# Two products with half as many stationary columns, an unrolled loop and a fifth mask on GpSimd in a four-layer graph kernel

## What is computed

```python
# layer 2, per head
logits = q @ k.T / sqrt(32) + log(clip(adj, 1e-8, None))
attn   = softmax(logits);  out = attn @ v
# layer 3, per head
logits  = q @ k.T / sqrt(32) + (2 * adj - 1)
weights = softmax(logits) * (0.25 + 0.75 * adj)
weights = weights / sum(weights);  attended = weights @ v
```

## Time and profile before

| | |
|---|---|
| median of three runs | 4772.2 us (4770.67 to 4772.46) |
| profiled execution, its own time | 4770.8 us |
| its span, first to last instruction | 4769.0 us |
| TensorE busy | 4307.2 us, 90% |
| VectorE busy | 3509.2 us, 74% |
| ScalarE busy | 2024.3 us, 42% |
| GpSimd busy | 1895.1 us, 40% |
| L618, 4096 records | 1132.9 us busy |
| L597 and L584, 2048 each | 659.2 and 657.1 us busy |
| L1324 on GpSimd, 512 | 1303.5 us busy, 2547 ns each |
| L1055 on VectorE, 512 | 767.3 us busy, 1501 ns each |

### The profile page before, as it was taken

How to read it: one execution, slowest core, us unless ns; L and a number is a source line. 1 busy time by engine, 2 the same in 40 slices (tenths; PEclk the granted TensorE clock), 3 DMA queues, 4 the chain that set the end, 5 groups by cost and what they waited for, 6 DMA issues and landing times.

```text
span 4769.0 us, 60615 instructions
## 1 busy us (share of the span) xinstructions
PE 4307.2 (90%) x16432; PEld 2005.4 (42%) x16432; DVE 3509.2 (74%) x4722; ACT 2024.3 (42%) x3638; POOL 1895.1 (40%) x1064
## 2 busy tenths in 40 slices
PE   7998899988999889998899898998989989899898
PEld 5523264232743337432374323743237332463324
DVE  3798748987489864898648986488855888558893
ACT  3264432544335443354423644235442354424543
POOL 1164602646026450264502645036440365404553
PEclk9998999989999899998999999999999999999999
DMA  3201102011020110201101011110111101111010
GB/s 104 67 18 32 49 23 59 18 32 49 25 59 16 34 47 28 56 16 34 47 32 53 15 34 47 33 53 14 36 47 34 49 14 36 49 36 47 14 35 16
DMA packets 109021, 179.63 MB, mean 38 GB/s; under 512 B 28256, under 2 KB 51040, under 8 KB 108704
## 3 DMA queue, kind: packets, MB, share of 16 engines
q1 hardware_dynamic: 108704, 175.89, 12.8%
HBM read 83.12 MB, written 8.39 MB: 19 GB/s over the span
## 4 chain that ended last, share of the span: by engine, by line
PE 59%; issue 17%; POOL 14%; DVE 7%; ACT 2%; POOLq 0%; DMA 0%; SPq 0%; DVEq 0%; ACTq 0%
PE ps L618 11%; PE ps L514 11%; POOL region_p L1324 9%; PE ps L560 9%; PE ps L506 8%; PE ps L597 6%; PE ps L584 6%; PE ps L707 5%; PE ps L550 2%; DVE row_max L1063 2%; POOL rstd L1336 1%; POOL v_head L1318 1%; DVE region_p L1055 1%; DVE sums_t L1034 1%; POOL y_t L1389 1%
## 5 line engine op out<-in xcount | busy, mean ns | idle before, releaser
L1324 POOL TENSOR_TENSOR region_p<-region_p,mask 128x1024 f32<-128x1024 f32 x512 | 1303.5, 2547 | 733.8 <-ACT region_p L827 733.6
L827 ACT ACTIVATE region_p<-ps 128x512 f32<-128x512 f32 x2048 | 1111.3, 595 | 907.8 <-PE ps L584 905.5
L1063 DVE TENSOR_REDUCE row_max<-ps 128x1 f32<-128x1024 f32 x1024 | 1213.5, 1214 | 42.7 <-PE ps L597 41.6
L618 PE MATMUL ps<-region_p,v_head 128*64 128x512 f32 x4096 | 1132.9, 634 | 74.4 <-POOL region_p L1324 30.2
L1055 DVE TENSOR_TENSOR region_p<-region_p,mask 128x1024 f32<-128x1024 f32 x512 | 767.3, 1501 | 67.3 <-ACT region_p L827 66.3
L597 PE MATMUL ps<-region_k,region_q 96*128 (+1 forms) x2048 | 659.2, 411 | 57.8 <-DVE row_max L1063 53.1
L584 PE MATMUL ps<-region_q,region_k 97*128 (+1 forms) x2048 | 657.1, 401 | 3.7 <-ACT region_p L827 1.1
L560 PE MATMUL ps<-values,region_k 128*128 128x256 f32 x2048 | 475.7, 387 | 0.0
L1336 POOL TENSOR_TENSOR rstd<-var_eps,minus_half 128x2 f32<-128x2 f32 (+1 forms) x160 | 119.5, 747 | 880.1 <-DVE var_eps L1015 880.1
L597 PEld LDWEIGHTS ps<-region_k,region_q 96*128 (+1 forms) x2048 | 130.1, 100 | 723.4 <-issue 459.6
L618 PEld LDWEIGHTS ps<-region_p,v_head 128*64 128x64 f32 x4096 | 208.9, 138 | 520.2 <-issue 393.4
(11 more groups left out here) (148 smaller groups left out, 4493.6 us busy)
## 6 DMA issues: line engine op xcount, KB each, us to landing
mask<-in_adj SPq DMA_DIRECT2D x64, 512.0 KB, 7.8
mask<-in_adj_t SPq DMA_DIRECT2D x64, 512.0 KB, 3.2
y_t<-o_raw SPq DMA_DIRECT2D x256, 64.0 KB, 2.0
sums_t<-o_raw SPq DMA_DIRECT2D x256, 64.0 KB, 2.0
region_q<-region_p SPq DMA_DIRECT2D x192, 64.0 KB, 2.0
region_k<-region_p SPq DMA_DIRECT2D x192, 64.0 KB, 2.0
region_q<-sums_t SPq DMA_DIRECT2D x192, 64.0 KB, 2.0
region_k<-sums_t SPq DMA_DIRECT2D x192, 64.0 KB, 2.0
```

The source lines that it names most:

```text
L618: last = nc.tensor.matmul(ps[64 * c:64 * c + 64, 6 + i, :], v_head[i][:, t, :], probs[:, t % RING, c * HALF:(c + 1) * HALF], start=(t == 0 ...
L827: nc.scalar.activation(probs[:, t % RING, c * HALF:(c + 1) * HALF], ps[:, 4 + c, :], ACT.Exp, scale=DK ** -0.5).then_inc(exp_done, 1)
L1063: nc.vector.tensor_reduce(row_max[i][:, t:t + 1], flat[:, (t % 2) * N:(t % 2 + 1) * N], AX.X, ALU.max)\
L1324: nc.gpsimd.tensor_tensor(p, p, mask[:, t, :], ALU.mult).then_inc(masked_pool, 1)
```

## The change

Both kinds of score product are split into two of 64 stationary columns, one for PSUM partitions 0 to 63 and one for 64 to 127, with the same moving operand. TensorE's loop over pairs of heads becomes unrolled code; the loops of the other engines stay. GpSimd masks tiles 0, 2, 3, 5 and 7 and VectorE tiles 1, 4 and 6; the copy of the next head's values so comes after tile 2. Which mask `with_values` and `make_mask3` wait for follows from the two tuples.

```diff
-POOL_TILES = (1, 3, 5, 7)
+POOL_TILES = (0, 2, 3, 5, 7)
...
                         pe.wait_ge(exp_done, att(b, layer, h, 2 * T, 2 * t + c - 1))
-                        nc.tensor.matmul(ps[:, 4 + c, :], k_aug[0:AUG, number(h), t * P:(t + 1) * P],
-                                         q_aug[0:AUG, number(h), c * HALF:(c + 1) * HALF],
-                                         start=True, stop=True).then_inc(st_done, 1)
+                        for m in range(2):
+                            last = nc.tensor.matmul(ps[64 * m:64 * m + 64, 4 + c, :],
+                                                    k_aug[0:AUG, number(h), t * P + 64 * m:t * P + 64 * m + 64],
+                                                    q_aug[0:AUG, number(h), c * HALF:(c + 1) * HALF],
+                                                    start=True, stop=True)
+                        last.then_inc(st_done, 1)
...
                 for c in range(2):
-                    last = nc.tensor.matmul(ps[:, 2 * (t % 2) + c, :], q_aug[0:AUG - 1, number(h), t * P:(t + 1) * P],
-                                            k_aug[0:AUG - 1, number(h), c * HALF:(c + 1) * HALF],
-                                            start=True, stop=True)
+                    for m in range(2):
+                        last = nc.tensor.matmul(ps[64 * m:64 * m + 64, 2 * (t % 2) + c, :],
+                                                q_aug[0:AUG - 1, number(h), t * P + 64 * m:t * P + 64 * m + 64],
+                                                k_aug[0:AUG - 1, number(h), c * HALF:(c + 1) * HALF],
+                                                start=True, stop=True)
                 last.then_inc(nat_done, 1)
...
-                with pe.Fori(1, H // 2 - 1) as pair:
+                for pair in range(1, H // 2 - 1):
                     for i in range(2):
                         head(b, layer, (pair, i), i, True)
```

## The result

The changed kernel takes 4710.9 us, median of four runs (4708.0 to 4715.6), against 4772.3 before (4770.7 to 4773.1). The ratio is 0.9874, 95% interval 0.9861 to 0.9887. The forecast was 4710 us. The profiled execution took 4708.0, its span is 4706.2, 62.8 less than before.

What follows compares the result with a forecast made beforehand. TensorE was taken to bound six of eight heads, VectorE and GpSimd the last two. 5.1 + 0.5 - 0.7 - 1.05 gave 3.9 us a layer, x 16 = 62 off 4772.2: 4710 us, range 4670 to 4750.

Steps and rivals of the forecast that it cites:

- five heads: Steady heads of an eight-head layer: each goes from 16.23 to 15.20 us, stall of 0.62 included; 5.1 a layer won.
- head 0: A layer's first head: three steps lack value products, five save 0.235 each, less a stall of 0.62; 0.5 us won.
- start of a layer: 64-column score products alternating with 128-column L506: 4 x 0.235 more, some 0.2 hidden by a VectorE wait; +0.7 us.
- last two heads: End of a layer, bounded by VectorE and GpSimd: +2.1 us in the first layer, 0 in the second.
- The step: TensorE's work per 128-row tile: 1.98 to 1.745 us, the 0.235 where 128 and 64 columns meet gone.
- The loads: Stationary loads of the split products, doubled in number: exposure taken as nothing, bounds nothing and 0.06 us a pair.
- (c): Doubled loads in front of split products make a pair 0.276 and the step 1.98 again: 4799 us; chance 0.11.
- (d): Gap around L618 comes from something else of fp32 on 64 columns and stays: about 4790 to 4800 us; chance 0.05.
- (e): Split bf16 score halves run one after the other, 2.59 us a step: about 5250 us; chance 0.03.
- (b): GpSimd's copy takes 0.9 us, two maxima are late, a head comes to 15.75: 4756 us; chance 0.08.
- (a): TensorE sets the pace throughout, no maximum is late, a head takes 14.57 us: 4647 us; chance 0.12.
- Cost of unrolling: zero: TensorE's unrolled loop over pairs of heads: no cost, bounds 0 and 1.0 us a layer, 16 in all.

Runs made afterwards that it cites:

- experiment 2: Kernel before the change with GpSimd masking tiles 0, 2, 3, 5, 7, nothing else: 4801.4 us, ratio 1.0051.
- experiment 4: Changed kernel with GpSimd masking tiles 1, 3, 5, 7 and the scores for the maximum whole again, only transposed scores split: 4758.1 us, ratio 0.9969.
- experiment 9: Changed kernel with GpSimd masking tiles 1, 3, 5, 7 and both halves for the maximum written to PSUM partitions 0 to 63: 4929.6 us, one run.
- experiment 1: Kernel before the change with TensorE's loop over pairs of heads unrolled, nothing else: 4749.9 us, ratio 0.9956.
- experiment 5: Changed kernel with ScalarE's fourth preparation of a next mask placed after tile 7 of the eighth head, not tile 6: 4694.9 us, ratio 0.9837.
- experiment 6: Changed kernel with GpSimd masking tiles 1, 3, 5, 7 and the split products for the maximum ordered m outside, c inside: 4647.7 us, ratio 0.9736.

## Why the prediction was right, and where it was not

**The sum.** Per layer, by the table of stretches:

| term | forecast | measured (first, second layer) |
|---|---|---|
| five heads | -5.15 | -5.02, -5.06 |
| head 0 | -0.5 | -0.76, -1.55 |
| start of a layer | +0.7 | +1.05, +1.10 |
| last two heads | +2.1, 0 | +3.06, +0.21 |
| net, mean of both | -3.9 | -3.49 |

Over the 16 layers that is -80.6 for -82 in the five heads, -18.5 for -8 in head 0, +17.2 for +11 at the start and +26.2 for +17 in the last two heads: -56 for -62, and 7 us from stretches that the sum didn't touch. Every term has the sign that was forecast, and the errors of the smaller ones cancel in part. That the total meets 4710 within 1 us is luck.

In medians, unrolling alone is -23.6, the splits on top of it -97.7 and the fifth mask on top of both +58.8 (-62.5; the change itself is -61.4). These parts hold for this order only. The 20 us that unrolling wins in the tails are there with four masks and not with five: with five masks the tails are 35.9 and 30.9 in the loop (experiment 2) and 36.3 and 31.1 unrolled (the changed kernel).

**The step** was forecast at 1.745 and is 1.73. The gap went where the forecast had it: 0.43 into the value product instead of 0.52, 0.86 out of it instead of 1.01, and experiment 4 shows nearly all of it (0.22) as soon as one kind of product has 128 columns again. That both kinds had to be split together was right. The loads of the stationary operand show what happens at the change of columns (before, then after):

```profile
477.01 0.20 PEld L618 LDWEIGHTS ps<-region_p,v_head 128*64 128x64 f32 x4 [0.42 <-issue]
```

```profile
465.53 0.36 PEld L623 LDWEIGHTS ps<-region_p,v_head 128*64 128x64 f32 x4
```

Before, the load for L618 starts together with its product (477.01), 0.31 after the last L584 has started. After, it starts 0.21 ahead of its product (465.74), while the product in front still runs. Out of the value product it is the same: the load and the product of L597 start together before (476.04 and 476.05), and the load of L601 runs 0.42 ahead after (466.18 and 466.60). In experiment 4 the load that isn't taken ahead is that of L585 (470.12, with its product), and L621's is again 0.21 ahead. At the border to L506 the load is 0.21 ahead before (404.61 for 404.82) and starts with its product after (403.89 for 403.90). At each of these changes of columns the load isn't taken ahead.

**Side by side** was taken from the fp32 value product alone; experiment 9 shows it for bf16. **The loads** cost nothing, as taken. The page's groups:

```profile
L601 PEld LDWEIGHTS ps<-region_k,region_q 96*64 96x64 bf16 x4096 | 204.8, 114 | 660.8 <-DVE row_max L1068 409.2 <-issue 211.2 <-DMA region_k<-region_p 14.3
L585 PEld LDWEIGHTS ps<-region_q,region_k 97*64 97x64 bf16 x4096 | 238.0, 113 | 383.5 <-ACT region_p L832 160.4
```

A half load takes 113 to 114 ns, the whole one took 102. Two of them one after the other, 0.23 a pair, would be more than the 0.216 of the products. They aren't taken one after the other: 4096 loads of 114 ns would be 467 us, and L601's are busy for 204.8, so the two halves' loads run at once. The Trainium skill (TensorEngine Tiling (Array Packing), Restrictions and Gotchas) has it that column tiling turns off fast weight load. The trace agrees in sign only: the load is 11 ns longer for half of the columns, but not the 138 of the fp32 one, and no run shows a cost of it. Rivals (c), (d) and (e) fell with the step; (b) had two late maxima a head, and there is one; (a) had none behind VectorE's stretched mask, and even with four masks the head stops at 14.97, not 14.57, since VectorE's queue is full.

**The head** came out at 15.18 for 15.20, with the one stall of 0.58 for 0.62 behind VectorE's mask of tile 4, as laid out. The rules read from the earlier trace rows (a VectorE mask and a GpSimd mask exclude each other, reductions from PSUM and GpSimd masks don't) carried it. No run tests them other than through such durations.

**Unrolling** is a term that failed, by a small amount. "Cost of unrolling: zero" had a bound for a loss and none for a gain. The some 0.21 between L605 and L597, which the forecast took as the transpose's own time, held 0.06 to 0.07 of the loop. That is 5 us, and the changed kernel has them. The 20 us of the tails in experiment 1 go with the granted clock, and the changed kernel doesn't have them. Whether the split products could have stayed in the loop wasn't tried.

**The last two heads of the first layer** were mis-sized twice. The earlier trace rows is from graph 0, and there the tail is 31.77; in six of eight graphs it is 33.7, because ScalarE's wait of experiment 5 is in them already. These are the graphs in which the clock is full in the middle of the tail; graphs 0 and 7 have neither the full clock nor the wait. The trace of before has it in a later graph (the columns are those of the timeline):

```profile
2115.62 1.15 ACT L815 ACTIVATE mask_exp<-mask,minus_ones 128x1024 f32<-128x1024 f32 x1 [2.31 <-DVE mask L1045]
```

"All eight look alike" was an assumption. In experiment 1 the wait is in no graph (31.8 in six of eight), but unrolled code doesn't remove it by itself: experiment 4 is unrolled and has it in seven of eight graphs, at 1.9 to 2.1 us, with a mean clock of 0.86 in the same stretch and the half clock a little later in it. With the fifth mask it is in all eight and longer, 4.47 for 2.31, and the forecast's working had only VectorE's and GpSimd's queues in it, not ScalarE's. From step 0 of the seventh head the forecast had 34.96 to 37.1; it was 36.9 to 39.4 in the typical graph, so the difference of 2.1 was near 2.5 with both ends wrong. **The second layer** was 34.2 in the forecast and is 34.14 (516.38 to 550.52), GpSimd's masks without a gap:

```profile
525.03 24.43 POOL L1329 TENSOR_TENSOR region_p<-region_p,mask 128x1024 f32<-128x1024 f32 x8
```

Eight masks at 3.05 each: one alone takes 2.36, so each spends some 0.7 behind VectorE's. That this tail costs nothing is in part the clock again: in the stretch from 14 to 26 us after the last transpose it is 0.72 in seven of eight graphs before and 1.00 in all after. With four masks and a full clock there is one graph, in experiment 4, and its tail is 28.7, not 31. How the zero divides between the mask and the clock isn't shown.

**The start** cost 1.1 instead of 0.7. The rows that answer to the earlier trace rows:

```profile
402.91 1.05 PE L601 MATMUL ps<-region_k,region_q 96*64 96x512 bf16 x8 [0.20 <-DMA region_k<-region_p]
403.90 2.00 PE L506 MATMUL ps<-w_v,y_t 128*128 128x256 f32 x8
405.82 0.62 PE L601 MATMUL ps<-region_k,region_q 96*64 96x512 bf16 x4
406.63 0.62 PE L601 MATMUL ps<-region_k,region_q 96*64 96x512 bf16 x4 [0.18 <-DVE row_max L1068]
```

The way out of L506 is 1.92 for 1.73, the way in 0.99 for 0.87: 0.31 for both, four times a layer 1.2, where 0.235 was taken from another pair of products. The wait for VectorE went from 0.52 to 0.18, which hides a part of it, as forecast.

**Head 0** won more than forecast in both layers; nothing was tried on it, and it stays open.

## What to carry to other kernels

Where products with 64 and with 128 stationary columns alternate, count the switches and measure both directions; splitting pays only if it removes all of them in the loop, and costs at every border that stays. Move work between VectorE and GpSimd by what a pair costs when they meet, not by busy shares, and divide it anew for stretches in which another engine has gone quiet. Before a tail is priced from one graph, read it in three, with every engine that has a queue there, and with the granted clock: a gain in a tail can be a half clock that falls elsewhere and keeps two masks apart.

## What the runs showed of the hardware that was not expected

- The two halves of TensorE's columns work through their products each at its own pace: the order of the halves doesn't matter (experiment 6), two products for the same half cost 0.216 each (experiment 9).
- The switch between 64 and 128 stationary columns costs 0.24 us there and back among the score products and the value product (0.09 and 0.15), 0.31 around the fp32 projection L506. The load behind the switch starts with its product and not 0.21 ahead of it.
- A half clock on TensorE can make a stretch shorter: the first layer's tail is 33.7 us at a granted clock of 1.00 in its middle and 31.9 at 0.72, in one and the same kernel.
- TensorE's products in a loop with addresses from a register start 0.06 to 0.07 later behind a transpose than unrolled ones (0.22 and 0.15, in the trace of before).
- GpSimd's copy of 32 value columns (L1318, now L1323) was mostly waiting. The two pages' groups, before and after:

```profile
L1318 POOL COPY v_head<-values 128x256 f32 (+1 forms) x128 | 146.9, 1147 | 497.2 <-ACT values L788 497.2
```

```profile
L1323 POOL COPY v_head<-values 128x256 f32 (+1 forms) x128 | 50.8, 397 | 500.1 <-ACT values L793 500.1
```

Moved from behind tile 3 to behind tile 2, it meets no VectorE mask any more and takes 0.40 also with an address from a register, which was rival (b)'s doubt.
